# A causal attention layer on one core: block products, rotary products and sums' parts at other row blocks

## The chip, the cores and the metric

The kernel runs on one core of a Trainium2 chip. Its time is the device time of one execution in microseconds (us), here the median of three runs. The engines are TensorE (PE, matmuls, with PEld for its weight loads), VectorE (DVE), ScalarE (ACT), GpSimd (POOL) and SyncE (SP), which issues the DMA transfers. Each takes its instructions in a fixed order, and semaphores hold an instruction until another engine has done its part.

## The reference

```
xn  = layernorm(x)                            # x: 1 x 2048 x 512, fp32
q   = xn @ wq        -> 16 heads x (128 + 64 rotary)
kva = xn @ wkv_a     -> ckv (128), k_pe (64, shared by the heads)
k, v = rmsnorm(ckv) * kvs @ wkv_b             # 16 heads x (128 + 128)
q_pe, k_pe = rope(q_pe), rope(k_pe)
attn = softmax(causal(concat(q, q_pe) . concat(k, k_pe) * scale))
out  = x + (attn @ v) @ wo + xn @ sum(factors) / sqrt(8) + bias
```

## The kernel before

**Units and row blocks.** The queries are taken in four chunks of 512 tokens, the last chunk first, and a chunk is a pass over the 16 heads. A unit `i` (0 to 63) is a head of a pass: pass one is units 0 to 15, pass two 16 to 31, and so on. Causality makes a pass shorter than the one before: up to four pieces of 512 keys in pass one, three, two and one after it. A unit has four row blocks `r` of 128 queries. In each, PE makes the scores of all pieces (five matmuls a piece, L753 to L759), then the fill work that `fills(i, r)` (L155) lists, in the order of its list. DVE takes each piece's maximum (L1454, the masked last piece L1456), combines them (L1466) and makes the offset `nm` (L1473); ACT takes the exponential (L1043) and its fp16 high part (L1053); POOL makes the low part (L1783); SP transposes both into `pT`. PE multiplies `pT` with the values in the next unit (`pv`, L557 to L559 with pT and vH or vL), in its last row blocks.

**Heads' outputs.** When a unit's `pv` is complete, ACT writes `oT` high (L1060), and at the start of the next unit DVE writes `oT` low (L1492), behind that row block's maximum. Only then can PE begin the output products `out` (wV<-oT, three matmuls), one in each row block of a unit; DVE adds each to `acc` (L1507).

**Queries from pass two on.** For two heads `g` (units 2g and 2g+1), `q` is built from seven block products of 256 columns, six matmuls each (L557 to L559 with wS), by a scheme with fewer products than blocks. In odd unit 2g-1 these are m1, m2, m6, m5, m3; in even unit 2g m7 and m4. m1, m6, m5 and m3 accumulate in one bank of PSUM, and ACT copies it out (a snapshot, L1015) after m1, m6 and m5; the next of them waits on PE for that copy. c11, c12, c22 and c21 are the four quarters of q: a high part by ACT (L1022 for c12, L1026) and a low part by DVE (L1431 for c12) or POOL (L1745). DVE adds m2, m7 and m4 to the snapshots (L1426).

**Rotary part.** `pe` (q_rope) is a product of twelve 512-column matmuls in an even unit for the next two; DVE turns it with three instructions (rot, L1441 to L1443) and POOL adds them (L1749). `parts` (rope_parts) makes the fp16 halves of each unit: ACT L1032, then two POOL instructions (L1767). The rotation waits for the previous odd unit's parts (semaphore g_parts), since it overwrites what they read.

**PSUM.** Three banks go round among the fill products in the order of the lists (`bank_order`); m1's stays taken until the step named in `LEFT`.

**Sums of weights in pass one.** For each pair of heads, ACT (L1001) and POOL (L1675) make four sums of absorbed weights in high and low parts, which SP stores for the later passes.

## Time and profile before

| | |
|---|---|
| runs | 1640.11, 1644.47, 1651.82 us |
| median | 1644.47 us |
| profiled execution | 1645.56 us, its span 1643.7 us |
| mean granted clock of TensorE | 0.975 of full |
| busy share of the span | PE 92%, DVE 64%, ACT 62%, POOL 63% |

A busy share is an average over four passes. A timeline row gives a start, a length, and in brackets how long the engine had been idle and which instruction ended that; "issue" there means that the profile shows no releaser, not that there was none. A matmul's length includes its way through the array, so the work of a run of matmuls is the distance from start to start.

### The profile page before, as it was taken

Reading aid. Unit: us, or ns where it says so; the run is one execution under the profiler, and the core shown is the slowest. Engines: PE = TensorE matmul, PEld = TensorE weight load, DVE = VectorE, ACT = ScalarE, POOL = GpSimd, SP = SyncE. Lnnn points to the kernel's source line nnn. Section 1 sums busy time; section 2 is a strip of 40 time slices with the busy share of each in tenths; the row PEclk is TensorE's granted clock in tenths of the full one; section 3 lists DMA queues with packets and bytes.
Section 4 is the critical chain, followed back from the end, with each engine's and each line's share of the span. In section 5 each row is a group of like instructions: output and inputs, shape, how many; then the busy total and the mean of one; then the engine's idle time right before and its main releaser. Section 6 shows DMA issues by size and latency. Waiting matters only on the chain.

```text
span 1643.7 us, 27314 instructions
## 1 busy us (share of the span) xinstructions
PE 1504.3 (92%) x8340; PEld 803.9 (49%) x8340; DVE 1052.0 (64%) x2627; ACT 1015.9 (62%) x2584; POOL 1038.0 (63%) x1081
## 2 busy tenths in 40 slices
PE   6899999999999989989898989888988888888887
PEld 5544555455555445444444544444444444445453
DVE  7778777777777656555555555555555555566666
ACT  7886777787775765555566656555455555444444
POOL 3788788775775975645677655565477655544453
PEclk9999999999999999999999999999999999999999
DMA  6599999987876886766666666656666656543444
GB/s 214 138 218 204 188 183 189 191 172 148 168 158 142 161 159 135 154 143 138 133 130 134 133 134 147 129 137 133 150 128 125 126 125 131 122 112 92 109 113 105
DMA packets 652256, 240.53 MB, mean 146 GB/s; under 512 B 599888, under 2 KB 614736, under 8 KB 651728
## 3 DMA queue, kind: packets, MB, share of 16 engines
q1 hardware_dynamic: 652112, 238.79, 67.7%
q8 instruction: 69, 1.13, 0.3%
q14 instruction: 75, 0.61, 0.1%
HBM read 75.10 MB, written 20.97 MB: 58 GB/s over the span
## 4 chain that ended last, share of the span: by engine, by line
PE 80%; issue 7%; DVE 6%; ACT 4%; POOL 1%; DMA 1%; SPq 0%; DVEq 0%; POOLq 0%; ACTq 0%
PE ps L557 16%; PE ps L559 15%; PE ps L558 15%; PE ps L753 7%; PE ps L754 6%; PE ps L755 6%; PE ps L758 6%; PE ps L759 6%; ACT ex L1043 2%; DVE gm L1454 1%; POOL st L1783 1%; DVE rden L1486 1%; DVE acc L1507 1%; DVE ps L1456 0%; ACT st L1053 0%
## 5 line engine op out<-in xcount | busy, mean ns | idle before, releaser
L1783 POOL TENSOR_TENSOR st<-ex,st 128x512 f16<-128x512 f32 (+3 forms) x640 | 638.9, 1017 | 514.6 <-ACT st L1053 506.9
L1043 ACT ACTIVATE ex<-ps,nm,scales 128x512 f32<-128x512 f32 (+3 forms) x640 | 452.9, 710 | 530.4 <-DVE nm L1473 529.9
L1454 DVE TENSOR_REDUCE gm<-ps 128x1 f32<-128x512 f32 (+1 forms) x384 | 249.3, 670 | 194.6 <-PE ps L759 191.6
L1053 ACT ACTIVATE st<-ex 128x512 f16<-128x512 f32 (+3 forms) x640 | 343.7, 565 | 6.4 <-ACT ex L1043 0.7
L1507 DVE SCALAR_TENSOR_TENSOR acc<-ps,rden,acc 128x512 f32<-128x512 f32 x256 | 190.2, 747 | 81.5 <-PE ps L559 80.7
L753 PE MATMUL ps<-kTh,q 128*128 128x512 f16 (+3 forms) x640 | 227.6, 356 | 8.1 <-ACT ex L1043 4.7
L754 PE MATMUL ps<-kTl,q 128*128 128x512 f16 (+3 forms) x640 | 227.6, 356 | 0.0
L755 PE MATMUL ps<-kTh,q 128*128 128x512 f16 (+3 forms) x640 | 227.5, 355 | 0.0
L758 PE MATMUL ps<-kRh,q 128*128 128x512 f16 (+3 forms) x640 | 226.7, 354 | 0.0
L759 PE MATMUL ps<-kRl,q 128*128 128x512 f16 (+3 forms) x640 | 225.3, 352 | 0.0
L557 PE MATMUL ps<-pT,vH 128*128 128x512 f16 (+3 forms) x640 | 222.8, 348 | 1.4 <-DMA pT<-st 1.4
L558 PE MATMUL ps<-pT,vH 128*128 128x512 f16 (+3 forms) x640 | 222.6, 348 | 0.0
L559 PE MATMUL ps<-pT,vL 128*128 128x512 f16 (+3 forms) x640 | 219.3, 348 | 0.0
L557 PE MATMUL ps<-wV,oT 128*128 128x512 f16 x256 | 100.0, 391 | 84.9 <-issue 84.6
L1767 POOL TENSOR_TENSOR q<-rot,q 32x512 f16<-32x512 f32 x128 | 147.3, 1151 | 16.7 <-POOL q L1745 5.2
L1456 DVE CUSTOM_DVE_ANT_0 ps<-ps,cmask 128x256 f32<-128x256 f32 (+3 forms) x256 | 133.2, 520 | 29.1 <-PE ps L759 25.7
L1043 ACT ACTIVATION_READ_ACCUMULATOR ex<-ps,nm,scales 128x1 f32 x640 | 126.4, 198 | 0.0
L753 PEld LDWEIGHTS ps<-kTh,q 128*128 128x128 f16 x640 | 64.0, 100 | 79.0 <-ACT ex L1043 14.4
L559 PE MATMUL ps<-wV,oT 128*128 128x512 f16 x256 | 101.6, 397 | 0.0
L558 PE MATMUL ps<-wV,oT 128*128 128x512 f16 x256 | 101.0, 395 | 0.0
L557 PEld LDWEIGHTS ps<-pT,vH 128*128 128x128 f16 x640 | 62.8, 98 | 65.4 <-issue 2.3
L754 PEld LDWEIGHTS ps<-kTl,q 128*128 128x128 f16 x640 | 63.9, 100 | 62.3 <-issue 6.7
(313 smaller groups left out, 2506.3 us busy)
## 6 DMA issues: line engine op xcount, KB each, us to landing
wS<-w_abs SPq DMA_DIRECT2D x48, 256.0 KB, 3.0
wV<-w_vo SPq DMA_DIRECT2D x48, 256.0 KB, 2.9
pT<-st SPq DMA_TRANSPOSE x640, 3.2
wS<-w_abs SPq DMA_DIRECT2D x24, 384.0 KB, 3.4
fland<-factors_in SPq DMA_DIRECT2D x28, 256.0 KB, 3.1
wP<-w_pe SPq DMA_DIRECT2D x24, 256.0 KB, 2.9
wsq<-wq_in SPq DMA_DIRECT2D x16, 256.0 KB, 3.7
wso<-wo_in SPq DMA_DIRECT2D x16, 256.0 KB, 3.0
```

The lines of the kernel that those rows point to most:

```text
L557: e.matmul(o, a[0], b[0], start=first, stop=False, skip_group_check=more)
L558: e.matmul(o, a[0], b[1], start=False, stop=False, skip_group_check=more)
L559: return e.matmul(o, a[1], b[0], start=False, stop=last, skip_group_check=more)
L753: e.matmul(b, q[:, i % 2, 0, qs], kTh[:, ks], start=True, stop=False)
L754: e.matmul(b, q[:, i % 2, 0, qs], kTl[:, ks], start=False, stop=False)
L755: e.matmul(b, q[:, i % 2, 1, qs], kTh[:, ks], start=False, stop=False)
L758: e.matmul(b, q[:, i % 2, 2, qs], kRh[:, ks], start=False, stop=False)
L759: e.matmul(b, q[:, i % 2, 2, qs], kRl[:, ks], start=False, stop=True).then_inc(z["p_s"], 1)
L1043: e.activation(ex[:, n % NEX, 0:keys], s_bank(n)[:, 0:keys], ACT.Exp, bias=nm[:, (i * QT + r) % 4:(i * QT + r) % 4 + 1], scale=scales[:, p ...
L1053: e.activation(stage(n, keys)[:, :, 0, :], ex[:, n % NEX, 0:keys].rearrange("p (t n) -> p t n", n=P), ACT.Copy).then_inc(z["a_pH"], 1)
L1454: e.tensor_reduce(m, b, AX_X, ALU.max).then_inc(z["v_max"], 1)
L1783: e.tensor_tensor(s[:, :, 1, :], ex[:, n % NEX, 0:keys].rearrange("p (t n) -> p t n", n=P), s[:, :, 0, :], ALU.subtract).then_inc(z["g_pL" ...
```

## The change

In odd units m2 and m6 are issued in row block 0 ahead of `out` (m6 was in 1, m2 behind `out`), m5 in 1, m3 in 2. c12's high part on ACT follows m3 in row block 2, its low part on DVE is in 3. In even units `pe` goes from row block 3 of unit e-2 to 0, ahead of `out`, and m4 goes behind `out`; a new step `rot` turns it in row block 2 on DVE and POOL, and the bank stays taken until then. ACT takes m1's snapshot ahead of the row block's exponentials. The ffn products move one unit on, and a pass's first rotary product keeps its place. In pass one the four high and four low parts of a pair's sums, which stood in a row, are spread over row blocks, S2 and S4 first, and their store comes later; for the first and the last pair they stay together. Semaphores and loads follow.

```diff
 PAIRS = tuple(QT * c // 2 + n for c in (ORDER[0],) + tuple(range(NC - 1)) for n in range(QT // 2))
 FFN = tuple(QT * c + t for c in ORDER for t in range(QT))
-FFN_UNITS = (H - 4,) + tuple(k * H + 4 for k in range(1, NC))
+FFN_UNITS = (H - 4,) + tuple(k * H + 5 for k in range(1, NC))
 ADDS = NF - KE
 SQUARED = 1 + ADDS // QT
...
-STEPS = {"p_m": ("m1", "m2", "m6", "m5", "m3", "m7", "m4"), "a_m": ("m1", "c11", "m6", "m5", "c12", "c22", "c21"),
+STEPS = {"p_m": ("m1", "m2", "m6", "m5", "m3", "m7", "m4"), "a_m": ("m1", "m6", "c11", "m5", "c12", "c22", "c21"),
          "v_m": ("c11", "c12", "c22", "c21"), "g_m": ("c11", "c22", "c21")}
...
 def token_slots(k):
-    return [(H - 3 + (n + 1) // QT, (n + 1) % QT) if k == 1 else ((k - 1) * H + 6 + n // 2, n % 2 * 2) for n in range(9)]
+    return [(H - 3 + n // QT, n % QT) if k == 1 else ((k - 1) * H + 6 + n // 2, n % 2 * 2) for n in range(9)]
 def sum_slot(m):
     return 2 * m - 1 if m else 0
+
+
+def sum_parts(m):
+
+    i = sum_slot(m) + 1
+    if m in (0, H // 2 - 1):
+        return [(i, 0)] * 4, [(i, 1)] * 4, (i, 2 if m == 0 else 1)
+    return [(i, 0), (i, 0), (i, 2), (i, 3)], [(i, 1), (i, 1), (i, 3), (i + 1, 0)], (i + 1, 0)
 SBANKS, OB, MB = 4, 4, 5
...
                 [("tq", 2), ("tkv", 2), ("q", 1), ("wpe_low", 2)], [("wabs", 2)]][r]
     if r == 1:
         if H <= i + 1 < NU and i % 2:
-            out += [("c11", (i + 1) // 2), ("m6", (i + 1) // 2)]
+            out.append(("c11", (i + 1) // 2))
         if H <= i < NU and i % 2 == 0:
-            out += [("c22", i // 2), ("m4", i // 2)]
+            out.append(("c22", i // 2))
     if r == 2:
-        if H <= i + 1 < NU and i % 2:
-            out.append(("m5", (i + 1) // 2))
         if H <= i < NU and i % 2 == 0:
             out.append(("c21", i // 2))
     if r == 0:
         if 1 <= i < H - 1:
             out.append(("q", i + 1))
         if H <= i + 1 < NU and i % 2:
-            out.append(("m1", (i + 1) // 2))
+            out += [(step, (i + 1) // 2) for step in ("m1", "m2", "m6")]
         if H <= i < NU and i % 2 == 0:
             out.append(("m7", i // 2))
+            if i + 2 < NU and (i + 2) % H:
+                out.append(("pe", i + 2))
         if 1 <= i <= H:
             out.append(("nv", i - 1))
         if i == SQUARED + 1:
...
             out.append(("tq", i + 2))
         if i // H == NC - 1 and i + 1 < NU and (i + 1) % H:
             out.append(("parts", i + 1))
-    if r == 0 and H <= i + 1 < NU and i % 2:
-        out.append(("m2", (i + 1) // 2))
+    if r and H <= i + 1 < NU and i % 2:
+        out.append(((None, "m5", "m3", "c12")[r], (i + 1) // 2))
+    if r == 1 and H <= i < NU and i % 2 == 0:
+        out.append(("m4", i // 2))
     if i in FFN_UNITS:
         out.append(("ffn", FFN_UNITS.index(i) * QT + r))
     if r == 1:
...
     if r == 2 and i and i % 2 == 0 and i + 2 < H:
         out.append(("wpe_low", i + 2))
     for e in range(2, NU, 2):
-        if (i, r) == pe_at(e):
-            out.append(("pe", e))
+        if (i, r) == pe_at(e) and (e < H or e % H == 0):
+            out += [("pe", e), ("rot", e)]
+        if e > H and e % H and (i, r) == (e - 2, 2):
+            out.append(("rot", e))
     if value_tiles(i, r) and i < NU:
         out.append(("pv", (i - 1, value_tiles(i, r))))
     if r == 2:
...
     for k in range(NC):
         if i == (k * H + 1 if k else 0):
             out.append(("bias", k * QT + r))
-    if r == 3 and H <= i + 1 < NU and i % 2:
-        out.append(("m3", (i + 1) // 2))
     for m in range(G0):
         if r == 3 and i == sum_slot(m):
             out.append(("sum", m))
-        if r == 0 and i == sum_slot(m) + 1:
-            out.append(("sum_hi", m))
-        if r == 1 and i == sum_slot(m) + 1:
-            out.append(("sum_lo", m))
+        high, low, _ = sum_parts(m)
+        out += [("sum_hi", (m, n)) for n in range(4) if high[n] == (i, r)]
+        out += [("sum_lo", (m, n)) for n in range(4) if low[n] == (i, r)]
     for k in range(1, NC):
         if (i, r) in token_slots(k):
             out.append(("tok", (k, token_slots(k).index((i, r)))))
...
 IN_BANKS = ("q", "pe", "tkv", "wvo", "tq", "wabs", "out", "ffn", "m1", "m2", "m7")
-LEFT = {"m1": "m3", "m7": "m4"}
+LEFT = {"m1": "c12", "m7": "m4", "pe": "rot"}
 LAST_READ = {"m1": "c12", "m2": "c11", "m7": "c21"}
...
             return 10 * (k - 1) + (3, 5, 8, 10)[n - 1]
+        def sum_part(m, n):
+
+            return (S2, S4, S3, S1)[n], weights_f(m, 0 if n < 2 else 1), slice(n % 2 * HC, n % 2 * HC + HC)
+
         snap = {"m1": kf[:, 0:HC], "m6": kf[:, HC:CH], "m5": wf[:, 0:HC]}
         def q_half(i, a, n):
...
                 elif h == 2:
                     e.wait_ge(z["g_kk"], NP)
                 elif h >= 3:
-                    e.wait_ge(z["g_sum"], 6 * m)
+
+                    e.wait_ge(z["g_sum"], 6 * m if h % 2 else 6 * m - 2)
                 e.activation(weights_f(m, h % 2), bank(("wabs", h)), ACT.Copy, scale=1.0 / WS).then_inc(z["a_wf"], 1)
-            def sums_high(m, which):
-
-                if which < 2:
+            def sums_high(m, n):
+
+                at, f, cols = sum_part(m, n)
+                if n < 2:
+                    e.wait_ge(z["g_sum"], 6 * m + 2)
+                else:
                     e.wait_ge(z["v_sum"], 2 * m + 2)
-                else:
-                    e.wait_ge(z["g_sum"], 6 * m + 2)
-                if m and which == 0:
+                if m:
                     e.wait_ge(z["d_sS"], 16 * m)
-                f = weights_f(m, 1 if which < 2 else 0)
-                if which < 2:
-                    parts = ((S3, slice(0, HC)), (S1, slice(HC, CH)))
-                else:
-                    parts = ((S2, slice(0, HC)), (S4, slice(HC, CH)))
-                at, cols = parts[which % 2]
                 e.activation(weight_block(at, 0), f[:, cols], ACT.Copy).then_inc(z["a_sum"], 1)
             def tokens_high(k, n):
...
                     for kind, n in fills(i, r):
                         if soon and kind == "pv" and n[0] < NU - 2:
                             fill(kind, n)
-                    early = ("q", "wo", "sqv", "m1", "c11", "m6", "c22") + (("sq1",) if i == 0 else ())
+                    early = ("q", "wo", "sqv", "m6", "c11", "c22") + (("sq1",) if i == 0 else ())
                     late = ("parts",) if last >= 2 and (r < 2 or i == 0) else ()
+                    for kind, n in fills(i, r):
+                        if kind == "m1":
+                            fill(kind, n)
                     for p in range(last + 1):
                         exps(i, r, p)
...
                     for kind, n in fills(i, r):
                         if soon and kind == "pv" and n[0] < NU - 2:
                             continue
-                        if last < 2 or (r >= 2 and i) or kind not in early + late:
+                        if kind != "m1" and (last < 2 or (r >= 2 and i) or kind not in early + late):
                             fill(kind, n)
...
                     weight_sums(n)
                 elif kind in ("m2", "m7", "m4"):
                     blocks_sum(kind, n)
-                elif kind == "m3":
+                elif kind == "c12":
                     block_low(n)
-                elif kind == "pe":
+                elif kind == "rot":
                     q_rope(n)
                 elif kind == "out":
                     head_output(n)
...
                 e.wait_ge(z["g_sum"], 6 * m + 1)
                 e.tensor_tensor(f0[:, HC:CH], f0[:, HC:CH], f0[:, 0:HC], ALU.subtract).then_inc(z["g_sum"], 1)
-            def sums_low(m):
-                f0, f1 = weights_f(m, 0), weights_f(m, 1)
-                if m:
-                    e.wait_ge(z["d_sS"], 16 * m)
-                for n, (at, f) in enumerate(((S3, f1[:, 0:HC]), (S1, f1[:, HC:CH]), (S2, f0[:, 0:HC]), (S4, f0[:, HC:CH]))):
-                    e.wait_ge(z["a_sum"], 4 * m + n + 1)
-                    e.tensor_tensor(weight_block(at, 1), f, weight_block(at, 0), ALU.subtract).then_inc(z["g_sum"], 1)
+            def sums_low(m, n):
+
+                at, f, cols = sum_part(m, n)
+                e.wait_ge(z["a_sum"], 4 * m + n + 1)
+                e.tensor_tensor(weight_block(at, 1), f[:, cols], weight_block(at, 0), ALU.subtract).then_inc(z["g_sum"], 1)
             def token_low(k, n):
                 e.wait_ge(z["a_tok"], 4 * (k - 1) + n)
...
                         if H <= i - 1 < NU:
                             load_vo(i - 1)
                     for m in range(G0):
-                        if (i, r) == (sum_slot(m) + 1, 2):
+                        if (i, r) == sum_parts(m)[2]:
                             store_sums(m)
-                    for kind, at, first in (("lA", (-2, 1), (-2, 1)), ("lS", (-2, 1), (-2, 3)), ("lB", (-1, 0), (-1, 0))):
+                    for kind, at, first in (("lA", (-2, 1), (-2, 1)), ("lS", (-2, 1), (-2, 2)), ("lB", (-1, 0), (-1, 0))):
                         for g in range(G0, 2 * NC * G0 // 2):
                             on = first if g == G0 else at
                             if (i, r) == (2 * g + on[0], on[1]):
...
                                 load_factor((r - 2) * KE + n)
                     if 1 <= i and KE + (i - 1) * QT + r + 2 < NF:
                         load_factor(KE + (i - 1) * QT + r + 2)
-                    if r == 2 and i % 2 and H <= i + 3 < NU:
+                    if r == (2 if (i + 3) % H == 0 or i < H else 0) and i % 2 and H <= i + 3 < NU:
                         load_pe(i + 3)
                     if r == 1 and h == H - 3 and k + 1 < NC:
                         e.wait_ge(z["v_pe"], (k + 1) * H // 2)
```

PE at the start of even unit 24: the end of the scores of row block 0, m7 (sqr,wS), the rotary product (fsum,wP) and the output (wV,oT). Before:

```order
L759 MATMUL ps<-kRl,q 128x256
L557 MATMUL ps<-sqr,wS 128x256 [waits s_d_lB,s_v_out]
...
L559 MATMUL ps<-sqr,wS 128x256
L557 MATMUL ps<-wV,oT 128x512 [waits s_d_lV0,s_v_o,s_v_out]
L558 MATMUL ps<-wV,oT 128x512
L559 MATMUL ps<-wV,oT 128x512
L753 MATMUL ps<-kTh,q 128x512 [waits s_a_exp]
```

And now:

```order
L772 MATMUL ps<-kRl,q 128x256
L570 MATMUL ps<-sqr,wS 128x256 [waits s_d_lB,s_v_out]
...
L572 MATMUL ps<-sqr,wS 128x256
L570 MATMUL ps<-fsum,wP 128x512 [waits s_d_lP,s_v_out]
L571 MATMUL ps<-fsum,wP 128x512
L572 MATMUL ps<-fsum,wP 128x512
...
L572 MATMUL ps<-fsum,wP 128x512
L570 MATMUL ps<-wV,oT 128x512 [waits s_d_lV0,s_v_o,s_v_m]
L571 MATMUL ps<-wV,oT 128x512
L572 MATMUL ps<-wV,oT 128x512
L766 MATMUL ps<-kTh,q 128x512 [waits s_a_exp]
```

Twelve rotary matmuls stand between m7 and the output, and the scores of row block 1 come behind both.

DVE in an even unit of pass three, from the offset of row block 2 (`nm`) over the output's addition to the offset of row block 3. Before:

```order
L1473 TENSOR_SCALAR nm<-rm,scales,head 128x1 [waits s_a_exp,s_v_rm]
L1507 SCALAR_TENSOR_TENSOR acc<-ps,rden,acc 128x512 [waits s_p_out,s_v_den,s_v_out]
L1454 TENSOR_REDUCE gm<-ps 128x1 [waits s_p_s]
L1456 ISA ps,gm<-ps,cmask 128x512 [waits s_p_s]
...
L1466 TENSOR_REDUCE rm<-gm 128x1 [waits s_v_max]
L1473 TENSOR_SCALAR nm<-rm,scales,head 128x1 [waits s_a_exp,s_v_rm]
L1507 SCALAR_TENSOR_TENSOR acc<-ps,rden,acc 128x512 [waits s_p_out,s_v_den,s_v_out]
L1441 TENSOR_TENSOR rot<-ps,tab 128x512 [waits s_g_parts,s_p_pe]
L1442 TENSOR_TENSOR rot<-ps,tab 64x512
L1443 TENSOR_TENSOR rot<-ps,tab 64x512
```

And now:

```order
L1484 TENSOR_SCALAR nm<-rm,scales,head 128x1 [waits s_a_exp,s_v_rm]
L1518 SCALAR_TENSOR_TENSOR acc<-ps,rden,acc 128x512 [waits s_v_den,s_p_out,s_v_out,s_v_ffn]
L1452 TENSOR_TENSOR rot<-ps,tab 128x512 [waits s_g_parts,s_p_pe]
L1453 TENSOR_TENSOR rot<-ps,tab 64x512
L1454 TENSOR_TENSOR rot<-ps,tab 64x512
L1465 TENSOR_REDUCE gm<-ps 128x1 [waits s_p_s]
L1467 ISA ps,gm<-ps,cmask 128x512 [waits s_p_s]
...
L1477 TENSOR_REDUCE rm<-gm 128x1 [waits s_v_max]
L1484 TENSOR_SCALAR nm<-rm,scales,head 128x1 [waits s_a_exp,s_v_rm]
L1518 SCALAR_TENSOR_TENSOR acc<-ps,rden,acc 128x512 [waits s_v_den,s_p_out,s_v_out,s_v_ffn]
```

The three rotation instructions, whose first waits for `g_parts`, stood behind row block 3's maximum and now stand ahead of it.

ACT in an odd unit of pass three, from the high parts of row block 2 to the next unit. Before, where L1015 is m5's snapshot and L1022 is c12:

```order
L1053 ACTIVATE st<-ex 128x4x128 [waits s_a_exp,s_d_pT4]
L1053 ACTIVATE st<-ex 128x3x128 [waits s_a_exp,s_d_pT5]
L1015 ACTIVATE wf<-ps 128x256 [waits s_g_m,s_p_m]
L1043 ACTIVATE ex,ssum<-ps,nm,scales 128x512 [waits s_g_pL,s_v_nm]
L1043 ACTIVATE ex,ssum<-ps,nm,scales 128x512 [waits s_g_pL]
L1053 ACTIVATE st<-ex 128x4x128 [waits s_a_exp,s_d_pT6]
L1053 ACTIVATE st<-ex 128x4x128 [waits s_a_exp,s_d_pT7]
L1060 ACTIVATE oT<-ps 128x512 [waits s_p_out,s_p_pv]
L1022 ACTIVATE q<-ps 128x256 [waits s_p_m]
L1043 ACTIVATE ex,ssum<-ps,nm,scales 128x384 [waits s_g_pL,s_v_den,s_v_nm]
```

And now, with c12 as L1031:

```order
L1062 ACTIVATE st<-ex 128x4x128 [waits s_a_exp,s_d_pT4]
L1062 ACTIVATE st<-ex 128x3x128 [waits s_a_exp,s_d_pT5]
L1031 ACTIVATE q<-ps 128x256 [waits s_p_m]
L1052 ACTIVATE ex,ssum<-ps,nm,scales 128x512 [waits s_g_pL,s_v_nm]
L1052 ACTIVATE ex,ssum<-ps,nm,scales 128x512 [waits s_g_pL]
L1062 ACTIVATE st<-ex 128x4x128 [waits s_a_exp,s_d_pT6]
L1062 ACTIVATE st<-ex 128x4x128 [waits s_a_exp,s_d_pT7]
L1069 ACTIVATE oT<-ps 128x512 [waits s_p_out,s_p_pv]
L1052 ACTIVATE ex,ssum<-ps,nm,scales 128x384 [waits s_g_pL,s_v_den,s_v_nm]
```

c12 stood at the unit's end, behind `oT`, and now stands ahead of the exponentials of row block 3.

## Rows read from the trace of the kernel before

**Rows 1.** The page: the chain that ended last, share of the span by engine.
```profile
PE 80%; issue 7%; DVE 6%; ACT 4%; POOL 1%; DMA 1%; SPq 0%; DVEq 0%; POOLq 0%; ACTq 0%
```

**Rows 2.** Windows, passes two, three, four: start, length, busy us of each engine, clock, DMA.
```profile
614.00:1062.00 448.00, 416.78 (x2219) 216.77 (x2217) 241.57 (x575) 265.01 (x665) 274.77 (x272) 0.97 0.67 137
...
1062.00:1408.00 346.00, 308.28 (x1705) 166.21 (x1703) 196.38 (x509) 186.03 (x479) 205.84 (x212) 0.96 0.60 131
...
1408.00:1643.00 235.00, 199.09 (x1179) 112.45 (x1179) 150.16 (x389) 106.93 (x275) 114.34 (x129) 0.94 0.45 110
```

**Rows 3.** Waits, whole span: who waited for whom: us, times, longest.
```profile
PE ps L557 <- issue: 84.6, 46, 3.6
...
PE ps L557 <- ACT ktmp L1015: 11.7, 15, 2.0
...
PE ps L753 <- ACT ex L1043: 4.7, 8, 1.6
```

**Rows 4.** Timeline of PE: start us, duration us, work, idle before it; passes two, three, four.
```profile
792.22 0.59 PE L557 MATMUL ps<-wV,oT 128*128 128x512 f16 x1 [3.13 <-issue]
...
819.77 0.38 PE L557 MATMUL ps<-wV,oT 128*128 128x512 f16 x1 [1.12 <-issue]
...
1241.79 0.38 PE L557 MATMUL ps<-wV,oT 128*128 128x512 f16 x1 [2.33 <-issue]
...
1545.37 0.38 PE L557 MATMUL ps<-wV,oT 128*128 128x512 f16 x1 [1.01 <-issue]
...
1559.23 0.38 PE L557 MATMUL ps<-wV,oT 128*128 128x512 f16 x1 [2.53 <-issue]
```

**Rows 5.** Timeline of PE: matmuls behind an even gap; a rotary product's first and last.
```profile
793.88 0.63 PE L754 MATMUL ps<-kTl,q 128*128 128x512 f16 x1
...
794.30 0.63 PE L755 MATMUL ps<-kTh,q 128*128 128x512 f16 x1
...
811.18 0.38 PE L557 MATMUL ps<-fsum,wP 128*128 128x512 f16 x1
...
813.55 0.38 PE L559 MATMUL ps<-fsum,wP 128*128 128x512 f16 x1
```

**Rows 6.** Timelines of PE, at odd unit 23's last output, and of DVE into unit 24.
```profile
782.90 0.38 PE L557 MATMUL ps<-wV,oT 128*128 128x512 f16 x1
...
789.13 0.43 DVE L1431 SCALAR_TENSOR_TENSOR q<-ps,q 128x256 f16<-128x256 f32 x1 [4.12 <-ACT q L1022]
...
791.43 0.68 DVE L1492 SCALAR_TENSOR_TENSOR oT<-ps,oT 128x512 f16<-128x512 f32 x1
```

**Rows 7.** Timeline of POOL: rotary parts of even units in passes two and three.
```profile
804.40 2.38 POOL L1767 TENSOR_TENSOR q<-rot,q 32x512 f16<-32x512 f32 x2 [0.17 <-POOL q L1745]
...
1251.24 2.37 POOL L1767 TENSOR_TENSOR q<-rot,q 32x512 f16<-32x512 f32 x2 [0.17 <-POOL q L1745]
```

**Rows 8.** Timelines: PE behind unit 40's scores of row blocks 1 and 3; DVE, a rotation.
```profile
1245.37 0.42 PE L557 MATMUL ps<-wsk,wS 128*128 128x256 f16 x1
...
1254.32 0.38 PE L557 MATMUL ps<-wV,oT 128*128 128x512 f16 x1
...
813.97 0.69 DVE L1441 TENSOR_TENSOR rot<-ps,tab 128x512 f32<-128x512 f32 x1 [1.32 <-PE ps L559]
```

**Rows 9.** Timeline of ACT, last row block of even unit 40 and behind it.
```profile
1255.82 0.78 ACT L1043 ACTIVATE ex<-ps,nm,scales 128x512 f32<-128x512 f32 x1 [2.77 <-DVE nm L1473]
...
1257.34 1.14 ACT L1053 ACTIVATE st<-ex 128x512 f16<-128x512 f32 x2
...
1259.39 0.60 ACT L1060 ACTIVATE oT<-ps 128x512 f16<-128x512 f32 x1 [0.91 <-PE ps L559]
...
1263.75 0.37 ACT L1015 ACTIVATE ktmp<-ps 128x256 f32<-128x256 f32 x1
```

**Rows 10.** Timeline of DVE, pass four, even unit: product of row block 2, offset of 3.
```profile
1537.81 0.74 DVE L1507 SCALAR_TENSOR_TENSOR acc<-ps,rden,acc 128x512 f32<-128x512 f32 x1
...
1539.38 0.27 DVE L1473 TENSOR_SCALAR nm<-gm,scales,head 128x1 f32<-128x1 f32 x1
```


## What the change should do to the time

> **What bounds the kernel now.** I read the chain of waits first: PE holds 80% of it [rows 1]. Then the windows: from unit 16 on, at 614 us, PE is busy 417 of 448, 308 of 346 and 199 of 235 us, at a granted clock of 0.97, 0.96 and 0.94 [rows 2]. So what can be won in the last three passes is PE's idle time and the time at the lower clock. The list of waits names two places: 46 waits of 84.6 us ahead of an output product and 15 of 11.7 us for a snapshot on ACT [rows 3]. The timeline shows where the 46 lie: at the first output product of a unit, 3.13 us in an even unit of pass two, 2.33 in pass three, 2.53 in pass four, and 1.12 to 1.01 in odd units [rows 4]. I counted them: 8 even ones in pass two's stretch (seven of 3.13, one of 3.61), 8 in pass three (seven of 2.33, one of 2.62), 6 in pass four; with the one of 3.96 us at unit 16 that is 63.6 us in even units, and 25 us in 23 odd ones.
>
> The even gaps cost a second time. Behind them 512-column matmuls start 0.42 us apart instead of 0.2155 (eleven spacings in 2.37 us), half clock, 1.2 instead of 2.4 GHz [rows 5]. Such stretches follow nearly every even gap and no odd one, 24 in all, some 3.3 us each, and lose 1.6 us each: 38.7 us in my count, within the 41 us that one minus the clock gives over the three windows [rows 2].
>
> Why is the even gap the longer? `out` waits for `oT` low on DVE, and DVE stood 4.12 us at c12's low part, whose high part ACT made only behind the last exponentials and `oT` [rows 6]. So the start of the next unit's maxima is late, and with it `oT`.
>
> **Even units, row block 0.** The rotary product, 12 x 0.2155 = 2.59 us, moves from row block 3 into the gap. c12 moves on ACT ahead of the exponentials, so DVE's wait of 4.12 us goes. From the end of an odd unit's scores of row block 3 (T) PE then has, in columns of 512 at 5 x 0.2155 for scores and 3 x 0.2155 for the others: output 0.65, values 1.63, scores 2.43 in pass two (1.36, 0.27 after), m7 0.65, rotary 2.59: T+7.95, T+6.9, T+5.8. In the trace the output started at 792.22 with T at 782.90 [rows 4, 6], T+9.3. With c12 gone DVE is done with the maxima about 1.1 us behind the scores and `oT` takes 0.68 [rows 6]; ACT's `oT` stands behind its last exponentials, T+6. So `oT` is there at about T+6.7 in pass two and earlier in the others, before PE is. All 63.6 us of even gaps go. What is late next there is nothing until row block 1; in pass four its output shares one bank with row block 0's and has only 0.54 us of scores ahead of it, where the addition on DVE takes 0.74 [rows 10] and two handovers: 0.45 us lost in seven units, -3.2.
>
> **Odd units, row block 0.** PE now has m1, m2, m6, `out`, 0.65 us each. The gap of 1.1 would be filled, but m6 waits for m1's snapshot, and ACT makes it only when it is through with row block 3 of the even unit: exponentials, high parts, `oT`. ACT needs from its first exponential of that row block to the end of the high parts 2.66 us in pass three, then 0.60 for `oT` and 0.37 for the snapshot, 3.6 together [rows 9]. And the exponentials wait for DVE's offset. That is the place where the change takes back what it gives.
>
> **The rotation.** Its three instructions of 0.69 us [rows 8], 2.07 together, now stand ahead of row block 3's maxima and wait for POOL's parts of the other unit. In pass three these end at 1253.61 [rows 7], 8.24 us behind the end of row block 1's scores (S = 1245.37, [rows 8]). PE, from S: output 0.65, m4 0.65, scores 1.89, output 0.65, values 2.59, scores of row block 3 2.16, which end at S+8.6. DVE starts the rotation at S+8.3, ends it at S+10.4, and has the offset, behind two maxima, at S+12.3; without the wait it would be S+10.1 (before, the exponential it released began at 1255.82, 1.5 us behind the scores' end at 1254.32, [rows 8, 9]). ACT's snapshot is then ready at S+15.9. PE reaches m6 at S+8.6+0.65+1.63+1.36+1.29 = S+13.5. So the gap of 1.11 becomes one of 2.35: 8 x 1.24 = 9.9 us lost. In pass four the parts come early, but between the output of row block 2 (ends at 1538.55) and the maximum of row block 3, over at 1539.65, there was no room [rows 10]: the rotation moves the offset 2.05 us on, and m6 comes 2.1 us late: 7 x 1.1 = 7.7 lost. In pass two POOL's parts end at 806.78 [rows 7] and row block 3 starts only 3 us later and has three pieces, so nothing moves; m6 waits 0.35 for ACT: 8 x 0.77 = 6.2 won. Odd units together: -11.4.
>
> **Snapshots.** 15 waits of 0.78 [rows 3]. m5's snapshot is now asked for in row block 2, when ACT is at the end of 1: I get 0.55 in pass three and 0.5 in four, 7.9 together: 3.8 won.
>
> **Clock.** Of 38.7 us all goes that followed even gaps. The 15 new odd gaps of 2.1 to 2.35 us are at most as long as the even ones of pass three, 2.33 us, behind which the clock fell seven times in eight, and in pass four shorter than any that it followed. I take half: 15 x 1.65 / 2 = 12.4 back, 26.3 won; ends 13.9 and 38.7.
>
> **Parts that cost nothing.** The load of `wP` goes out one row block behind the product that frees it and has a unit of 12 us or more until it is used; without that cover PE would stand at `pe` with `out` and all scores behind it. POOL's addition of the rotation ends before row block 3's low parts. The ffn products only change units. Pass one: the spreading touches ACT and POOL where PE waits for an exponential at most 4.7 us in the whole span [rows 3]; I take 0, from -2 to +4.
>
> **One rule against the trace.** The trace's spacing of 512-column matmuls is 0.2155 us [rows 5]. The Trainium skill, "TensorE: Matmul & The Clock Gate", section "Back-to-back issue gap", gives about 131 ns for a pair of weight load and matmul of 512 columns in a real kernel. By that twelve would cover 1.57 us of a gap, not 2.59, and 23 moved products 24 us less than I count: an estimate of 1590 in place of the sum below. No row here is that short, and I stay with 0.2155.
>
> **Sum.** 63.6 - 3.2 - 11.4 + 3.8 + 26.3 = 79.1 us. The profiled execution is 1645.56 (its span 1643.7 and 1.9 around it), so 1566.5; the median of the runs, 1644.47, is 1.1 lower, within their spread. I say 1567.
>
> **Rivals.**
> - The rotation does not hold DVE up (POOL's parts earlier than in the trace, as POOL's own waits shrink). For it: POOL mostly waits for ACT. Against: the parts follow low parts and c22 on POOL in a row, and pass four needs no wait to be late. Then the odd gaps fall to 0.35 and 0.1 and the clock stays: 16 + 14 + 12.4 more, 1524. Chance 0.08.
> - The chains give it back: with PE faster, ACT, POOL and the transposes run closer behind, and passes three and four keep their total idle time. For it: the odd gap shows this already. Against: ACT and POOL are busy 54 to 61% of the windows [rows 2]. Only pass two gains: 29.5 (even) + 6.2 + 13.6 (nine stretches of 1.5), about 1596. Chance 0.17.
> - A product covers only 1.57 us, as by the rule above. In rows: even gaps keep 1 us each, 1590. No row speaks for it; 0.01.
> - The steps change order but PE's time does not: the idle time only moves within the unit, 1645. Against: the rotary product leaves row block 3, and nothing there waited. Chance 0.04.
> - Slower: DVE in order with the rotation at its head. The wait for g_parts holds up the maxima, the offset, the exponentials, m1's snapshot, and so m6, `out` and the scores behind it on PE, once in each pair of units. A pair loses 5.8 to 5.9 us now (two gaps, a snapshot wait, a slow stretch; 2.33 + 1.12 + 0.79 + 1.65). With an odd gap g it would lose g + 1.65 + 0.55, which is more from g = 3.7 and 1% slower from 4.4, 2 us more than I get, in all passes. At g = 5 it is 23 x 1.35 = 31 us: 1676. For it: POOL's parts lie 8.2 us behind the scores. Against: ACT and DVE catch up within each unit. Chance 0.04.
>
> **Numbers.** Forecast 0.66: 1567, by itself from 1545 (all clock back, longer odd gaps partly covered) to 1590 (all new gaps slow the clock, 12.4, and 10 us of small waits). The range 1545 to 1605 takes in the second rival and the bounds of the clock; it leaves out the first, the fourth and the fifth, 0.16, and tails. A measurement of this kernel can tell about 1% from no change; faster by over 1% is below 1628: 0.66 + 0.08 + 0.17 + 0.01 = 0.92, less 0.01 for tails: 0.91; within 1% 0.05, slower 0.04.
>
> **What would show it.** In the timeline of PE: no idle time ahead of an even unit's first output; idle time ahead of m6, about 0.35, 2.35 and 2.1 us in passes two, three, four; the waits list names ACT's L1024 (the snapshot) as PE's largest, some 40 us, and not "issue". On DVE the first rotation instruction waits for POOL in pass three. DVE's wait of 4.12 us at c12 is gone. The clock is 1.0 in pass two and 0.96 to 1.0 after it. I am wrong if even gaps stay (then `oT` has another cause than c12), or if the odd gaps are short (then the rotation holds nothing).

## The result

The changed kernel takes 1535.97 us (median of four runs, 1534.08 to 1539.08) against 1643.53 us (1640.11 to 1651.82) for the kernel before: a ratio of 0.934, 95% interval 0.930 to 0.938. It is faster, as forecast, and by more: 1567 was forecast, and 1545 was the lower end of the forecast range. A second set of five runs, on another chip, had a median of 1537.03 us (`change_again` below). The profiled execution took 1535.01 us, with a span of 1533.2.

The chain of waits, by engine, answers to [rows 1]:

```profile
PE 44%; DVE 7%; ACT 6%; issue 3%; POOL 2%; DMA 0%; DVEq 0%; ACTq 0%; POOLq 0%; SPq 0%
```

The windows of passes two, three and four, with the columns of [rows 2]. A pass now begins at 608, 1010 and 1322 us:

```profile
608.00:1010.00 402.00, 399.81 (x2193) 211.84 (x2192) 242.60 (x575) 261.82 (x660) 272.89 (x272) 1.00 0.76 154
1010.00:1322.00 312.00, 295.91 (x1718) 164.45 (x1717) 195.54 (x510) 185.26 (x482) 205.86 (x212) 1.00 0.71 145
1322.00:1533.00 211.00, 187.90 (x1191) 108.48 (x1188) 146.13 (x389) 107.44 (x280) 114.80 (x130) 1.00 0.54 123
```

PE is busy 399.8 of 402, 295.9 of 312 and 187.9 of 211 us. The clock is 1.00 in all three, where it was 0.97, 0.96 and 0.94. The passes are shorter by 46, 34 and 24 us.

The waits of the whole span, which answer to [rows 3]; POOL's L1776 is `parts`, its L1754 the low part of c11 or c22, DVE's L1452 the first rotation instruction:

```profile
DVE rot L1452 <- POOL q L1776: 27.4, 13, 3.2
...
PE ps L570 <- ACT ktmp L1024: 19.5, 13, 2.0
...
PE ps L766 <- POOL q L1754: 5.5, 7, 3.3
...
PE ps L570 <- DVE acc L1518: 3.1, 8, 0.4
```

Of the 84.6 us in 46 waits ahead of the output products 2.5 us in three are left. The snapshot holds PE for 19.5 us, not for some 40. The timeline of PE shows where, in pass three (the first two rows) and pass four; wA,wS and fland,wS are m6, fsum,wS at 1314.19 is m3 of unit 47:

```profile
1071.03 0.28 PE L570 MATMUL ps<-wA,wS 128*128 128x256 f16 x1 [2.01 <-ACT ktmp L1024]
...
1314.19 0.28 PE L570 MATMUL ps<-fsum,wS 128*128 128x256 f16 x1 [1.37 <-ACT wf L1024]
...
1409.58 0.39 PE L570 MATMUL ps<-wV,oT 128*128 128x512 f16 x1 [0.41 <-DVE acc L1518]
...
1416.28 0.22 PE L766 MATMUL ps<-kTh,q 128*128 128x128 f16 x1 [0.40 <-POOL q L1754]
1419.35 0.28 PE L570 MATMUL ps<-fland,wS 128*128 128x256 f16 x1 [1.33 <-ACT ktmp L1024]
```

m6 waits 2.01 to 2.03 us six times in pass three, six times in pass four (1.25 to 1.33 us four times, 0.73 and 0.77 once each), once for 0.73 us at the end of pass one, and not once in pass two. m3 waits once, 1.37 us, in unit 47. Even gaps are left in two units only: 1.22 us in unit 30 and 1.07 us in unit 46. Into these two no rotary product was moved, since a pass's first one keeps its place, and the gaps are as long as in the kernel without the moved product (`blocks_alone`, below).

The chain of work that sets the wait in pass three can be read in one place, across the engines, from row block 1 of an even unit to m6 in the odd unit behind it. The output at 1055.06 starts where the scores of row block 1 end: that is S of the forecast.

```profile
1055.06 0.38 PE L570 MATMUL ps<-wV,oT 128*128 128x512 f16 x1
...
1060.93 2.38 POOL L1776 TENSOR_TENSOR q<-rot,q 32x512 f16<-32x512 f32 x2 [0.17 <-POOL q L1754]
...
1063.41 0.69 DVE L1452 TENSOR_TENSOR rot<-ps,tab 128x512 f32<-128x512 f32 x1 [3.17 <-POOL q L1776]
...
1067.24 0.27 DVE L1484 TENSOR_SCALAR nm<-rm,scales,head 128x1 f32<-128x1 f32 x1
...
1067.55 0.78 ACT L1052 ACTIVATE ex<-ps,nm,scales 128x512 f32<-128x512 f32 x1 [5.18 <-DVE nm L1484]
...
1070.12 0.59 ACT L1069 ACTIVATE oT<-ps 128x512 f16<-128x512 f32 x1
1070.59 0.38 ACT L1024 ACTIVATE ktmp<-ps 128x256 f32<-128x256 f32 x1
```

The rotation starts at S+8.35 (forecast S+8.3), the offset is there at S+12.45 (S+12.3), the snapshot at S+15.9 (S+15.9). So the chain came as forecast, and PE alone was later at its m6: its wait of 2.01 us began at S+13.96, not at S+13.5. Of these 0.45 us, 0.16 are only counting: the matmul ahead of m6 has a length of 0.27 us, the sum takes it at its spacing of 0.11, and the bracket begins at its end.

### The profile page after: what moved, and what is told of

It is laid out like the page before. It is cut to its first block, busy times and chain, and to the rows that moved or that the text cites. A ratio compares the mean times of both kernels' runs of the same rounds, so it can differ in the third digit from the quotient of the medians.

```text
span 1533.2 us, 27332 instructions
## 1 busy us (share of the span) xinstructions
PE 1465.0 (96%) x8340; PEld 794.8 (52%) x8340; DVE 1038.2 (68%) x2627; ACT 1011.1 (66%) x2584; POOL 1036.3 (68%) x1081
## 4 chain that ended last, share of the span: by engine, by line
PE 44%; DVE 7%; ACT 6%; issue 3%; POOL 2%; DMA 0%; DVEq 0%; ACTq 0%; POOLq 0%; SPq 0%
PE ps L570 9%; PE ps L572 9%; PE ps L571 9%; PE ps L766 3%; PE ps L772 3%; PE ps L767 3%; PE ps L771 3%; PE ps L768 3%; ACT ex L1052 3%; DVE ps L1467 2%; DVE acc L1518 1%; ACT st L1062 1%; POOL q L1776 1%; DVE gm L1465 1%; POOL st L1792 1%
## 5 line engine op out<-in xcount | busy, mean ns | idle before, releaser
L766 PE MATMUL ps<-kTh,q 128*128 128x512 f16 (+3 forms) x640 | 222.2, 347 | 13.5 <-POOL q L1754 5.5
L772 PE MATMUL ps<-kRl,q 128*128 128x512 f16 (+3 forms) x640 | 222.1, 347 | 0.0
L771 PE MATMUL ps<-kRh,q 128*128 128x512 f16 (+3 forms) x640 | 222.1, 347 | 0.0
L768 PE MATMUL ps<-kTh,q 128*128 128x512 f16 (+3 forms) x640 | 222.1, 347 | 0.0
L767 PE MATMUL ps<-kTl,q 128*128 128x512 f16 (+3 forms) x640 | 222.1, 347 | 0.0
L1776 POOL TENSOR_TENSOR q<-rot,q 32x512 f16<-32x512 f32 x128 | 147.1, 1149 | 18.0 <-POOL q L1754 5.3
L570 PE MATMUL ps<-wV,oT 128*128 128x512 f16 x256 | 97.1, 379 | 5.7 <-DVE acc L1518 3.1
L572 PE MATMUL ps<-wV,oT 128*128 128x512 f16 x256 | 97.0, 379 | 0.0
L571 PE MATMUL ps<-wV,oT 128*128 128x512 f16 x256 | 97.0, 379 | 0.0
L570 PEld LDWEIGHTS ps<-pT,vH 128*128 128x128 f16 x640 | 62.6, 98 | 62.6 <-issue 2.4
L571 PEld LDWEIGHTS ps<-pT,vH 128*128 128x128 f16 x640 | 62.6, 98 | 60.3
```

The lines of the kernel that those rows point to most:

```text
L570: e.matmul(o, a[0], b[0], start=first, stop=False, skip_group_check=more)
L571: e.matmul(o, a[0], b[1], start=False, stop=False, skip_group_check=more)
L572: return e.matmul(o, a[1], b[0], start=False, stop=last, skip_group_check=more)
L766: e.matmul(b, q[:, i % 2, 0, qs], kTh[:, ks], start=True, stop=False)
L767: e.matmul(b, q[:, i % 2, 0, qs], kTl[:, ks], start=False, stop=False)
L768: e.matmul(b, q[:, i % 2, 1, qs], kTh[:, ks], start=False, stop=False)
```

## The experiments

There are twelve, each with its expectation as it was noted before the kernel ran. The kernel before, run beside them, had medians of 1642.73, 1643.17 and 1641.0 us. Each has one profiled execution, and waits and clock are read from that one.

**The rotation one row block later.**

```diff
-        if e > H and e % H and (i, r) == (e - 2, 2):
+        if e > H and e % H and (i, r) == (e - 2, 3):
```

> The changed kernel (1536 us) with the rotation (rot, DVE and POOL) back in row block 3; the rotary product stays in row block 0 of the even unit. Theory: in row block 2 the rotation holds row block 3's maxima up, and with them ACT and m6; PE's waits of 2.0 us for m1's snapshot in pass three and 1.3 us in pass four go, and about 0.7 to 0.9 us ahead of the odd unit's first output come in their place, 0.5 us in pass two too: 9 + 5 us won, 4 lost, about 1525 us. Rival (ACT's own load makes the snapshot late, the rotation's place is indifferent or better where it is): the waits for the snapshot stay near 2.0 us and DVE's oT comes later, 1536 to 1546 us.

Measured: 1519.87 us (1519.85 to 1520.97), ratio 0.9255, interval 0.9241 to 0.9269. DVE's wait for POOL's parts has left the list. DVE, ACT and PE at the same place of the pass as above:

```profile
1060.36 2.38 POOL L1776 TENSOR_TENSOR q<-rot,q 32x512 f16<-32x512 f32 x2 [0.17 <-POOL q L1754]
...
1064.25 0.27 DVE L1484 TENSOR_SCALAR nm<-rm,scales,head 128x1 f32<-128x1 f32 x1
1064.56 0.78 ACT L1052 ACTIVATE ex<-ps,nm,scales 128x512 f32<-128x512 f32 x1 [2.76 <-DVE nm L1484]
1065.10 0.68 DVE L1452 TENSOR_TENSOR rot<-ps,tab 128x512 f32<-128x512 f32 x1
...
1067.13 0.59 ACT L1069 ACTIVATE oT<-ps 128x512 f16<-128x512 f32 x1
...
1068.28 0.27 PE L570 MATMUL ps<-wA,wS 128*128 128x256 f16 x1
```

From the end of POOL's parts to the offset it was 4.2 us and is now 1.8; `oT` starts 6.8 us behind the start of the parts instead of 9.2, and m6 (wA,wS) carries no bracket: PE does not wait. What is left there in pass three is 0.40 us ahead of the same unit's output, six times. Only the rotation's place was changed, and with it how long its bank stays taken. So the wait at m6 came down the chain from the rotation over the maxima, the offset, the exponentials and the snapshot, and the kernel is 16 us faster than the change.

**c12's high part on ACT behind the last exponentials again** (ahead of `oT`; in the kernel before it stood behind `oT`).

```diff
-                elif kind == "m3":
+                elif kind == "c12":
                     block_high("c12", n)
```

> The changed kernel with c12's high part on ACT behind the exponentials of row block 3 again (ahead of oT). Theory: DVE waits some 3.5 us for it once in each odd unit, oT comes at T+8.8 in pass two and behind the value products by 4.3 in pass four, so PE waits about 0.9 us in 9 even units and 0.8 us in 6, none in pass three: 1549 us. Rival (c12 was not what made oT late; the rotary product alone closes the even gap): 1536 us, no wait of DVE over 1 us there turns up on PE.

Measured: 1557.63 us (1555.95 to 1558.9), ratio 0.9482, interval 0.9467 to 0.9498. It costs 21 us, not 13. The waits (L1442 is c12's low part, L1031 its high part):

```profile
DVE q L1442 <- ACT q L1031: 75.9, 24, 5.5
...
PE ps L570 <- issue: 13.8, 15, 3.3
```

The snapshot's waits stayed (19.7 us). The output gaps are 11.3 us longer in all than in the change. With the rotary product in them, 0.71 us is left five times in pass two, nothing in the inner units of pass three and 0.6 us six times in pass four; 7.0 us stand at three pass edges (3.30, 1.18 and 2.50). The rest of the 21 us is 5.3 us more busy time of PE and single waits of 1.8 to 2.4 us more. So c12's late place is a cause of the even gap, and the rotary product covers most of what it makes.

**The rotary part of the change alone**, on the kernel before, with its ffn slot and its load; block products, c12 and sums as before.

```diff
         if H <= i < NU and i % 2 == 0:
             out.append(("m7", i // 2))
+            if i + 2 < NU and (i + 2) % H:
+                out.append(("pe", i + 2))
...
-        if (i, r) == pe_at(e):
-            out.append(("pe", e))
+        if (i, r) == pe_at(e) and (e < H or e % H == 0):
+            out += [("pe", e), ("rot", e)]
+        if e > H and e % H and (i, r) == (e - 2, 2):
+            out.append(("rot", e))
```

> The kernel before with the rotary product and its rotation moved as in the change (and the ffn products one unit on), the block products and the sums as before. Theory: even gaps close but for 0.7 us in pass two (57 us won, and 38.7 of clock), but the rotation in row block 2 delays the odd units' oT and nothing stands ahead of the output there: odd gaps of about 3.4 us in passes three and four, 2.3 more than before, 34 us lost, and a clock that falls behind them, 25 us: about 1607 us. Rival (the rotary product carries the gain, the block products are a trifle): 1550 us or less, odd gaps unchanged at 1.1 us.

Measured: 1603.07 us (1600.12 to 1606.31), ratio 0.976, interval 0.9739 to 0.9781. PE's waits, a window of pass three and a gap in it:

```profile
PE ps L561 <- issue: 55.6, 32, 3.2
```

```profile
1050.00:1280.00 230.00, 208.60 (x1165) 114.37 (x1163) 132.73 (x344) 126.99 (x329) 143.83 (x148) 0.96 0.63 136
```

```profile
1185.32 0.38 PE L561 MATMUL ps<-wV,oT 128*128 128x512 f16 x1 [3.17 <-issue]
...
1187.27 0.63 PE L757 MATMUL ps<-kTh,q 128*128 128x512 f16 x1
1187.69 0.63 PE L758 MATMUL ps<-kTl,q 128*128 128x512 f16 x1
```

In pass three the even gap is filled (in pass two 0.54 us is left of it) and the odd one has grown from 1.12 to 3.17 us. Eight us ahead of it DVE's first rotation instruction waits for POOL, as in the change:

```profile
1177.20 0.69 DVE L1445 TENSOR_TENSOR rot<-ps,tab 128x512 f32<-128x512 f32 x1 [3.18 <-POOL q L1771]
```

A slow stretch follows each of the six gaps of 3.17 us (scores 0.42 us apart): the clock of the window is 0.96.

**The block products and c12 alone**: the changed kernel with the rotary product, its rotation and its load in row block 3 as before.

```diff
-            if i + 2 < NU and (i + 2) % H:
-                out.append(("pe", i + 2))
...
-        if (i, r) == pe_at(e) and (e < H or e % H == 0):
-            out += [("pe", e), ("rot", e)]
-        if e > H and e % H and (i, r) == (e - 2, 2):
-            out.append(("rot", e))
+        if (i, r) == pe_at(e):
+            out += [("pe", e), ("rot", e)]
```

> The changed kernel with rotary product and rotation where they were before (row block 3 of the even unit); block products and sums as changed. Theory: c12's early high part shortens the even gaps to about 1.4, 1.2 and 1.0 us, short enough to leave the clock up; m2 and m6 fill the odd gaps and nothing delays them: 35 + 38.7 + 24 + 9 us won, about 1540 us, so most of the gain is here. Rival (the rotary product in the gap is what counts): even gaps stay above 2 us, the clock falls, 1600 us or more.

Measured: 1534.03 us (1532.62 to 1535.47), ratio 0.9337, interval 0.9321 to 0.9352: as fast as the whole change. The 23 waits ahead of an output product:

```profile
PE ps L566 <- issue: 25.0, 23, 2.3
```

```profile
710.55 0.38 PE L566 MATMUL ps<-wV,oT 128*128 128x512 f16 x1 [1.22 <-issue]
...
1181.29 0.38 PE L566 MATMUL ps<-wV,oT 128*128 128x512 f16 x1 [1.07 <-issue]
...
1455.65 0.38 PE L566 MATMUL ps<-wV,oT 128*128 128x512 f16 x1 [0.75 <-issue]
```

Its even gaps are 1.22, 1.07 and 0.75 us long instead of 3.13, 2.33 and 2.53, its odd ones are gone, m6 does not wait, and its clock is 0.997. So in the whole change the rotary part adds nothing: it fills all but 2.5 of these 25 us and gives them back at m6 (18.8 us) and in small waits of pass four.

**The wait ahead of m6, lengthened.** What decides when the clock falls? Empty copies (their result is used by nothing) on ACT ahead of m1's snapshot make the wait longer. The expectations speak of 8 waits in pass three; there are six. With one copy of 256 columns:

```diff
+                if kind == "m1" and 2 * H <= 2 * g - 1 < 3 * H:
+                    for width in (256,):
...
+                        e.activation(junk[:, 0:width], cmask[:, 0:width], ACT.Copy).then_inc(z["a_x"], 1)
```

> The changed kernel (1536 us, clock 1.00) with one idle copy of 256 columns on ACT ahead of m1's snapshot in the odd units of pass three, about 0.4 us: PE's wait ahead of m6 goes from 2.02 to 2.4 us, longer than the 2.33 us behind which the clock fell in the kernel before. Theory 1 (the gap's length decides, and 2.02 was only just short enough): the clock falls behind most of the 8 and each costs 1.65 us more: 1536 + 3 + 12 = about 1551 us, clock 0.96 in pass three. Theory 2 (2.4 us is not enough here, the fall needs more than the gap): 1539 us, clock 1.00.

Measured: 1539.05 us (1538.25 to 1539.85), six waits of 2.31 or 2.32 us. The 13 us behind the fourth and the fifth of them; the columns are those of [rows 2], the clock is the third number from the end:

```profile
1193.90:1207.00 13.10, 13.01 (x65) 6.72 (x66) 6.20 (x18) 9.18 (x25) 9.44 (x11) 0.87 0.70 156
1233.00:1246.00 13.00, 12.43 (x70) 6.76 (x71) 7.28 (x19) 8.57 (x25) 8.70 (x11) 1.00 0.75 158
```

A slow stretch of 3.4 us at half clock shows as 0.87 in such a window. It follows one of the six. With two copies of 512 columns (`for width in (512, 512)`):

> The changed kernel with two idle copies of 512 columns there, about 1.3 us: waits of about 3.3 us, as long as the 3.13 us of pass two before. Theory 1: the clock falls behind all 8: 1536 + 10 + 13 = about 1559 us. Theory 2 (the clock falls for another reason than this gap's length): 1546 us, clock 1.00.

Measured: 1553.63 us (1553.58 to 1553.69), waits of 3.19 us. The 13 us behind the third and the fourth:

```profile
1164.00:1177.00 13.00, 12.84 (x64) 6.73 (x65) 6.26 (x17) 9.29 (x26) 8.57 (x10) 0.87 0.84 158
1204.00:1217.00 13.00, 12.37 (x70) 6.69 (x71) 7.06 (x18) 9.66 (x27) 10.10 (x12) 1.00 0.84 158
```

Five of six windows show 0.87, this fourth one does not. With one copy of 512 columns (`for width in (512,)`):

> The changed kernel with one empty ScalarE copy of 128x512 ahead of the snapshot of product m1 in every odd unit of pass three, so the snapshot, and with it the end of TensorE's wait for m6's accumulator, comes later. The wait was 2.02 us without a filler (no clock fall in 8), 2.32 us with a 256-column one (one fall in 8) and 3.19 us with two of 512 columns (a fall behind all of them). Expected wait here: about 2.6 us. Theory A: the clock falls from a length between 2.32 and 2.6 on, and each of the 8 waits costs 0.6 us more of length and some 1.2 to 1.7 us of clock: 1537 + 4.8 + 11 = 1553. Theory B: the length from which it falls lies between 2.6 and 3.19, as at most one of 8 here: 1537 + 4.8 + 1 = 1543, with a granted clock of 0.99 or more over 980 to 1295 us.

Measured: 1543.66 us (1542.13 to 1545.19), six waits of 2.52 or 2.53 us, slow stretches behind two of them. Its time is that of its theory B, though with two falls and not one. At this place a fall thus followed one wait of 2.32 us, two of 2.52 us and five of 3.19 us, of six each, one execution for each length. (The expectation of this run has all of the longest; one of them had none.) For 2.01 to 2.03 us there are four profiled kernels with six such waits each: the change, its second profile, the one with c12 late and the one with the sums' parts in a row. One of these 24 was followed by a fall, in the last of the four:

```profile
1078.43 0.28 PE L568 MATMUL ps<-wA,wS 128*128 128x256 f16 x1 [2.02 <-ACT ktmp L1022]
```

```profile
1079.00:1092.00 13.00, 12.91 (x64) 6.44 (x62) 6.31 (x18) 7.62 (x22) 7.37 (x9) 0.87 0.67 156
```

**The same at the even gap.** In the kernel before, a gap of 2.33 us was followed by a fall six times in seven (the forecast's seven in eight counts the gap of 2.62 us at the end of the pass in). Is it the place that decides? The kernel with the blocks alone, and two empty copies ahead of the `oT` of pass three's odd heads:

```diff
+                if 2 * H <= i < 3 * H and i % 2:
+                    for width in (512, 512):
...
+                        e.activation(junk[:, 0:width], cmask[:, 0:width], ACT.Copy).then_inc(z["a_x"], 1)
```

> The kernel of blocks_alone (1534.0 us; wait ahead of the even units' rotation product 1.07 us in pass three) with two empty ScalarE copies of 128x512 ahead of the eviction of the output tile in pass three's odd units, so that the wait ahead of the even units' rotation product grows to about 2.3 us, as long as it was in the kernel before, and at the same product. Theory A: what decides whether the clock falls is where the wait stands (what TensorE did ahead of it and does behind it), and the fall comes behind 7 of 8 as in the kernel before: 1534 + 8 x 1.2 + 7 x 1.65 = 1555 us, clock 0.96 in pass three. Theory B: the length alone decides, and at 2.3 us the fall comes once in 8, as at the wait ahead of m6: 1534 + 9.6 + 1.7 = 1545 us, clock 0.99 or more.

Measured: 1534.11 us (1533.04 to 1535.18), as without the copies, and the gaps kept their length: 2.30 us at the first of the pass, 1.07 at the seven others. The copies stand at the wrong `oT`. ACT writes the `oT` of an odd head at the end of the even unit behind it, ahead of the odd gap, which m1, m2 and m6 fill in this kernel. The output that waits in the even gap needs the `oT` of the even head, and ahead of that one (at 1059.12 us, with the gap at 1060.59) there is no copy:

```profile
1076.51 1.29 ACT L1072 ACTIVATE junk<-cmask 128x512 bf16<-128x512 bf16 x2 [0.91 <-PE ps L568]
```

So whether the place decides is not tested. But the first gap tells something: it stands in both kernels, ahead of all copies, and behind it the clock fell with the blocks alone and did not fall here. The gap and the 13 us behind it, first with the blocks alone:

```profile
1021.32 0.38 PE L566 MATMUL ps<-wV,oT 128*128 128x512 f16 x1 [2.29 <-issue]
```

```profile
1022.00:1035.00 13.00, 13.00 (x62) 6.32 (x60) 6.78 (x18) 6.25 (x17) 7.70 (x9) 0.88 0.64 137
```

And with the copies:

```profile
1021.59 0.38 PE L566 MATMUL ps<-wV,oT 128*128 128x512 f16 x1 [2.30 <-issue]
```

```profile
1021.00:1034.00 13.00, 12.41 (x65) 6.34 (x66) 7.54 (x21) 7.50 (x21) 9.18 (x10) 1.00 0.83 144
```

So the same gap at the same product is followed by a fall in one execution and not in another. The gap of 2.09 us at the start of pass four does the same: at 1328 us there is a fall with the blocks alone and none with the copies.

**The sums' parts in a row again.**

```diff
-    if m in (0, H // 2 - 1):
-        return [(i, 0)] * 4, [(i, 1)] * 4, (i, 2 if m == 0 else 1)
-    return [(i, 0), (i, 0), (i, 2), (i, 3)], [(i, 1), (i, 1), (i, 3), (i + 1, 0)], (i + 1, 0)
+    return [(i, 0)] * 4, [(i, 1)] * 4, (i, 2 if m < H // 2 - 1 else 1)
```

> The changed kernel with the sums' four high and four low parts of pass one in a row again (ACT in one row block, POOL in the next, the store in the third). Theory: the spreading is what took away the two waits of 2.2 us ahead of a norm product in pass one (161 and 299 us before) and kept them away: about 1541 us. Rival (they went by the new order of the parts or by chance): 1536 us, no such waits.

And the changed kernel once more, on the same chip:

> The changed kernel itself on the same chip, to compare with: 1536 us, whatever the theory.

Measured: 1539.99 us (1536.42 to 1545.08) with the parts in a row and 1537.03 us (1536.0 to 1538.89) with them spread; by time alone these can't be told apart. The waits can: with the parts in a row PE waits twice in pass one for DVE's `oT` (at 229.57 and 301.10 us), as it did in the kernel before (2.24 and 2.19 us), and with them spread this row is absent.

```profile
PE ps L619 <- DVE oT L1501: 4.2, 2, 2.1
```

The clock fell behind both waits, though they are 2.13 and 2.12 us long; the clock is 0.87 behind the first,

```profile
229.00:242.00 13.00, 12.43 (x57) 6.59 (x58) 9.00 (x25) 9.46 (x23) 7.17 (x7) 0.87 0.84 197
```

and the same behind the second. In the kernel before it fell behind neither. The medians differ by 3.0 us, of which the waits alone would make 4.2.

**m4 ahead of the output in pass four**, on the kernel with the later rotation, and that kernel again.

```diff
+            if i >= (NC - 1) * H:
+                out.append(("m4", i // 2))
...
-    if r == 1 and H <= i < NU and i % 2 == 0:
+    if r == 1 and H <= i < (NC - 1) * H and i % 2 == 0:
```

> The kernel of rot_back (1519.9 us) with block product m4 ahead of the output product, in row block 1 of the even units of pass four. There the output product waited 0.41 us for VectorE's sum in the accumulator's bank, seven times; m4 is some 1 us of TensorE's work that needs nothing of it. Theory: the wait is covered, 1519.9 - 7 x 0.4 = 1517.0 us, the waits of 0.4 us gone from the list. Rival: m4 itself waits there for the snapshot or its own bank, and the time stays at 1520 or goes to 1523, with a new wait at m4.

> The kernel of rot_back again, beside m4_first on the same chip, so that 3 us between them can be told from none. Theory: 1519.9 us within 1 us, with the same waits (none at m6 in passes two and three, 0.16 to 0.41 us in pass four).

Measured: 1518.8 us (1517.59 to 1520.33) and 1520.8 us (1520.0 to 1524.3). The output's waits for DVE's sum fall from 3.1 to 0.3 us, but the scores of the next unit's row block 0 wait longer for the low part of q: seven waits, 5.5 us together and six of them of some 0.4 us or less, became

```profile
PE ps L768 <- POOL q L1756: 8.9, 7, 3.3
```

The six are now up to 0.99 us long: the wait has moved on, from row block 1 of the even unit to the start of the odd one. The output's waits and these together make 9.2 us instead of 8.6, so by them nothing is won. The medians are 2 us apart and the runs of the two overlap, so the times don't settle it. These two kernels are the fastest here, at 1519 to 1521 us.

## Why it came out faster than forecast

The direction and the mechanism were right; two terms of the sum failed in size, both the same way, and the range missed by 9 us. The forecast was 1564.6 us for the span and it is 1533.2, so 31.4 us are to be explained. PE's idle time was forecast at 86.6 us (139.4 before less 52.8) and is 68.2 (1533.2 less 1465.0 busy): 18.4 of them. PE's busy time fell by 39.3 us where 26.3 were given to the clock: 13.0.

**Even units, row block 0: right but for two gaps.** Of the 63.6 us, 2.3 are left, in units 30 and 46. I said that all go, and had not seen that no rotary product comes into these two (it is also 21 products that move, not the 23 of the estimate by the page's rule). With the blocks and c12 alone the even gaps shrink to less than 25 us. The loss of 0.45 us at pass four's second output is there, 0.41 us.

**The rotation: right in its mechanism, too long in its size. This step failed.** Its instructions, the offset and the snapshot came within 0.15 us of the forecast instants. PE reached m6 some 0.3 us later than I summed, 0.25 of it in a pause ahead of the next unit's first scores that I had not counted. I gave pass three eight waits of 2.35 us and there are six of 2.02: 18.8 against 12.1 us. Unit 46 has no moved rotation, so seven were possible; in unit 32 DVE waits for POOL too (3.17 us), but m6 behind it does not wait, and why is open. Pass four: seven of 2.1, 14.7, against 6.7 us in six. Of the difference some 0.4 us each time is PE's wait for POOL's low part of q, which stands between the last scores and m6 (1416.28 and 1419.35 above) and so comes off the wait at m6; the rest is open. Pass two: 2.8 against nothing. Less the 0.7 at the end of pass one that is 17 us together.

**Snapshots: too long in size.** I forecast 7.9 us of waits at m3 and there is one of 1.4. In pass three m5's snapshot ends at 1078.06 and m3 starts at 1078.12: 0.06 us decided, since PE comes later there than I reckoned.

**Clock: this step failed.** I let half of the 15 new odd gaps slow the clock, because I took their length for the cause, by seven falls behind eight gaps of 2.33 us. It was six behind seven, and one behind a gap of 2.62. The new gaps came out at 0.73 to 2.03 us, and in the profiled execution none of the twelve was followed by a fall: the 12.4 us that I gave back stayed won. A length of 2.02 us does not keep the clock up by itself. It fell behind one of 24 such waits at this place, and in two other kernels behind a snapshot wait of the same 2.02 us (at 1395.27 us in the kernel before, at 1358.88 us with the rotary part alone). The lower end, 1545, had all of the clock won and counted on some 10 us less of waits; 18.4 us less of idle time is what left it.

**Pass one: taken as nothing, 4 us won.** The sums' parts in a row on ACT had held up `oT` and with it a norm product on PE, two waits of 2.2 us.

**What I left out** goes the other way: seven waits for POOL's low part of q in pass four's scores, 5.5 us where there was 1.0 (3.28 of them in the last one, near the kernel's end), and three output gaps, those of units 30 and 46 and one of 0.17 (2.5). 17 + 6.5 + 4 less these 7.0 is 20.5, against the 18.4 of the two idle times; the 2 us between them I can't place.

**What a moved product covers: right.** The rotary product's first matmul and the output behind its twelve, in an even unit of pass three:

```profile
1050.19 0.38 PE L570 MATMUL ps<-xT,wP 128*128 128x512 f16 x1
...
1052.78 0.38 PE L570 MATMUL ps<-wV,oT 128*128 128x512 f16 x1
```

They are 2.59 us apart, 12 x 0.2155, as summed, and the output has no wait in front. The rival of 1.57 us is refuted. The rule of the Trainium skill, "TensorE: Matmul & The Clock Gate", section "Back-to-back issue gap", of about 131 ns for a pair of weight load and 512-column matmul, does not agree with this trace.

**The rivals.** "The rotation does not hold DVE up", 1524, was false for the change and is what rot_back makes true: 1520. "The chains give it back", 1596, was false: PE's idle time fell from 37.7 to 16.1 us in pass three and from 35.9 to 23.1 in pass four, and so was "the idle time only moves", 1645. The slower one had the right chain; its price is in rotary_alone, where the odd gap did come to 3.17 us, below the 3.7 from which it would have lost, and that kernel is faster than before by 40 us. In the change the wait stays at 2.02 us; that m2, which stands ahead of m6 there, and m1's snapshot ahead of the exponentials keep it so short is argued and no run tests it.

## What to carry to other kernels

When a product on PE is moved into a gap, look at what the move makes the other engines do in their fixed order. The same move of the rotary product was worth nothing with its rotation in row block 2 (1534 us without the move, 1536 with it) and 14 us with the rotation one row block later (1520), with PE's own work the same. And look for who is late before filling the gap: one copy of 0.4 us on ACT (c12), a block of exponentials too late, cost 21 us even with the rotary product in the gap. Count the places, too: a step that a pass's edge leaves out is missing there from what is won and from what is lost. A cost that comes or stays away, such as the slow clock, is better carried as two outcomes, each with its own sum, than as their half.

## What the runs showed of the chip

Behind a wait of 3.19 us the granted clock is at 1.2 GHz for some 3.4 us and then back at 2.4: 256-column matmuls start 0.21 us apart, and 0.11 once it is over. The rows are of the kernel with two copies of 512:

```profile
1073.10 0.40 PE L570 MATMUL ps<-wA,wS 128*128 128x256 f16 x1 [3.19 <-ACT ktmp L1034]
1073.29 0.42 PE L571 MATMUL ps<-wA,wS 128*128 128x256 f16 x1
...
1077.25 0.27 PE L767 MATMUL ps<-kTl,q 128*128 128x256 f16 x1
1077.36 0.27 PE L768 MATMUL ps<-kTh,q 128*128 128x256 f16 x1
```

Unexpected was that the same gap in the same program is followed by the fall only in a share of cases. Ahead of m6 in pass three the share was one of 24 at 2.02 us, one of six at 2.32, two of six at 2.52 and five of six at 3.19; the last three are one execution each, so the order is clear only between the ends. At other places the length tells less: 2.33 us ahead of an output brought six falls in seven in the kernel before, 2.12 and 2.13 us ahead of a norm product brought two of two with the sums' parts in a row, and 2.19 and 2.24 us at such products none of two in the kernel before. What decides besides the length stays open.
